# Two operations a tile for the heads of layers 1 and 2, score columns in ScalarE's copy, and new orders of work

## The reference

```
h = jnp.maximum(_layernorm(x), 0.0)
x = x + _L1_gnn_ref(h, adj, W, a)
#   h = (x @ W).reshape(.., 4, 64); e = leaky_relu(s_src[:, :, None] + s_dst[:, None])
#   att = softmax(where(adj > 0, e, MASK)); h_prime = einsum('bijh,bjhd->bihd', att, h)
```

## Time and profile before

| | |
|---|---|
| time, median of 3 runs | 4377.15 us (4377.02 to 4380.96) |
| the profiled execution | 4382.13 us, span 4380.3 us |
| PE busy | 4104.0 us, 94% |
| DVE busy | 3246.0 us, 74% |
| ACT busy | 2163.2 us, 49% |
| POOL busy | 417.4 us, 10% |
| mean granted TensorE clock | 0.969 |

### The profile page before, as it was taken

One profiled execution on the slowest core, in us unless ns is written; L12 is line 12 of the kernel. 1 busy time (PEld: TensorE's weight loads), 2 busy tenths in 40 slices (PEclk: granted clock), 3 DMA queues, 4 the chain that ended last, 5 costly groups with the idle time before them and its releaser, 6 DMA issues.

```text
span 4380.3 us, 59537 instructions
## 1 busy us (share of the span) xinstructions
PE 4104.0 (94%) x22884; PEld 1923.7 (44%) x22884; DVE 3246.0 (74%) x6985; ACT 2163.2 (49%) x3361; POOL 417.4 (10%) x469
## 2 busy tenths in 40 slices
PE   5799999999999999999999999999999999999987
PEld 2344444344444444444444444444444444444443
DVE  5577777877777877777877777877777877777854
ACT  3344455544455544455544455544455544555532
POOL 0001010101110100110100110100110100110100
PEclk9899999999999999999999999999999999999998
DMA  3111211111111111101111111112101121101000
GB/s 101 29 35 54 54 40 34 48 40 54 54 33 41 35 54 54 54 30 44 35 54 54 54 30 44 34 54 54 54 29 45 35 54 54 53 26 39 25 30 29
DMA packets 212314, 193.92 MB, mean 44 GB/s; under 512 B 144448, under 2 KB 179008, under 8 KB 203584
## 3 DMA queue, kind: packets, MB, share of 16 engines
q1 hardware_dynamic: 212032, 190.12, 15.3%
HBM read 138.95 MB, written 17.56 MB: 36 GB/s over the span
## 4 chain that ended last, share of the span: by engine, by line
PE 57%; DVE 30%; ACT 5%; SPq 3%; DMA 2%; issue 2%; POOL 1%; DVEq 0%; ACTq 0%; POOLq 0%
PE M L422 10%; PE M L435 9%; DVE PG L1017 6%; DVE PP L903 6%; PE M L488 5%; PE M L446 4%; DVE x L934 4%; PE O L474 4%; PE S L355 4%; PE O L537 4%; DVE Q L913 4%; DVE PP L1046 3%; PE M L579 3%; PE O L368 2%; SPq L1181 2%
## 5 line engine op out<-in xcount | busy, mean ns | idle before, releaser
L1017 DVE SCALAR_TENSOR_TENSOR PG<-g,tcg,mT 128x512 f32<-128x512 f32 x1024 | 694.3, 743 | 36.0 <-PE O L478 17.0
L622 ACT ACTIVATE PP<-S,reach 128x1024 f32<-128x1024 f32 x512 | 542.4, 1110 | 238.6 <-PE S L355 189.2
L903 DVE TENSOR_TENSOR PP<-PP,mT 128x1024 f32<-128x1024 f32 x512 | 597.7, 1214 | 32.0 <-ACT PP L622 32.0
L474 PE MATMUL O<-PG,V 128*32 128x512 f32 x4096 | 536.5, 643 | 10.7 <-DVE PG L1017 9.3
L647 ACT ACTIVATE z<-x,nb,rs 128x256 f32<-128x256 f32 x384 | 209.2, 597 | 540.1 <-DVE nb L893 540.1
L422 PE MATMUL M<-hT,W 128*128 128x512 f32 x1024 | 456.0, 598 | 5.1 <-ACT hT L657 2.0
L435 PE MATMUL M<-W,H 128*128 128x256 f32 x2048 | 459.7, 378 | 0.0
L1128 POOL TENSOR_SCALAR ve<-mv 128x4 f32<-128x4 f32 x192 | 111.3, 580 | 3409.3 <-DVE mv L861 3409.3
L979 DVE TENSOR_TENSOR x<-x,M 128x256 f32<-128x256 f32 x128 | 52.6, 411 | 490.5 <-PE M L435 490.4
L435 PEld LDWEIGHTS M<-W,H 128*128 128x128 f32 x2048 | 377.3, 189 | 71.6 <-issue 10.6
L355 PE MATMUL S<-hT 32*128 32x512 f32 x2048 | 325.6, 707 | 56.3 <-ACT PP L622 28.4
(11 more groups left out here) (136 smaller groups left out, 5511.2 us busy)
## 6 DMA issues: line engine op xcount, KB each, us to landing
g<-t_rows SPq DMA_DIRECT2D x64, 1024.0 KB, 5.1
adj<-adj_in SPq DMA_DIRECT2D x32, 1024.0 KB, 5.4
x<-x_in SPq DMA_DIRECT2D x32, 512.0 KB, 4.3
z<-t_rows SPq DMA_DIRECT2D x64, 256.0 KB, 4.0
out<-x SPq DMA_DIRECT2D x32, 512.0 KB, 2.9
W<-w_in SPq DMA_DIRECT2D x1, 3072.0 KB, 16.5
mT<-z SPq DMA_TRANSPOSE x128, 3.7
m<-V SPq DMA_TRANSPOSE x128, 2.5
```

The source lines that it names most:

```text
L474: e.matmul(k.O[0][r:r + 32, :], s.V[:, jt, 64 * hh + 32 * v:64 * hh + 32 * v + 32], p[:, u, :], start=(jt == 0), stop=(jt == NT - 1))
L622: e.activation(p[:, 2 * pair:2 * pair + 2, :], k.S[:, 2 * pair:2 * pair + 2, :], ACT.Exp, bias=k.reach[:, 7:8], scale=SC0).then_inc(k.e0.s ...
L903: e.tensor_tensor(p[:, 2 * pair:2 * pair + 2, :], p[:, 2 * pair:2 * pair + 2, :], s.mT[:, jt:jt + 1, :].to_broadcast([128, 2, N]), ALU.mul ...
L1017: e.scalar_tensor_tensor(out=p[:, u, :], in0=s.T[hh], scalar=s.tcg[:, 1, hh, jt:jt + 1], in1=s.mT[:, jt, :], op0=ALU.max, op1=ALU.mult).th ...
```

## The change

The scaled heads of layers 1 and 2 go into V in one instruction a tile, and fin adds V to x in another. V gets 264 columns a row, the last 8 are stt, and ACT's copy of a projected tile takes all 264; DVE's copy is gone. Waits of DVE on itself (diag, zb) use its own chain counter in place of signals. The landings of layers 1 and 2 share a semaphore. The five orders are rewritten: b0 now stands for what was b1, and so on.

```diff
-            s.V = sb(f"V{k}", [128, NT, D])
+            vs = sb(f"V{k}", [128, NT, D + 8])
+            s.V, s.stt = vs[:, :, 0:D], vs[:, :, D:D + 8]
+            s.vs = vs[:, :, :]
-            s.mk = s.V[:, :, :].rearrange("p t d -> p (t d)").bitcast(BF16).rearrange("p (t n) -> p t n", t=NT)
+            s.mk = vs[:, :, :].bitcast(BF16)[:, :, 0:N]
...
+    def nth(self, b, i):
+        return self.sems[b % self.n], 16 * (self.per * (b // self.n) + i + 1)
...
@@ class Pe, b2r
-        self.take(f"M{t % 2}", k.add[L].at(b, t) if L else k.nrm.at(b, t))
+        self.take(f"M{t % 2}", k.nrm[L].at(b, t))
@@ class Pe, pj
-        self.take(f"M{t % 2}", k.pjs[L].at(b, t))
+        self.take(f"M{t % 2}", k.pjc[L].at(b, t))
@@ class Act, pj
-        e.copy(s.V[:, t, :], k.M[t % 2][:, 0:256]).then_inc(k.pjc[L].sem, 1)
+        e.copy(s.vs[:, t, :], k.M[t % 2][:, 0:264]).then_inc(k.pjc[L].sem, 1)
@@ class Dve, b2r
-        if L:
-            for h in range(4):
-                x = s.x[:, t, 64 * h:64 * h + 64]
-                r = e.scalar_tensor_tensor(out=x, in0=M[:, 64 * h:64 * h + 64], scalar=s.ri[:, t, h:h + 1], in1=x,
-                                           op0=ALU.mult, op1=ALU.add)
-            r.then_inc(k.add[L].sem, 1)
-        else:
-            e.tensor_tensor(s.V[:, t, :].rearrange("p (h d) -> p h d", d=32), ...
+        n = 4 if L else 8
+        e.tensor_tensor(s.V[:, t, :].rearrange("p (h d) -> p h d", h=n), M[:, 0:256].rearrange("p (h d) -> p h d", h=n),
+                        s.ri[:, t, 0:n, None].to_broadcast([128, n, D // n]), ALU.mult).then_inc(k.nrm[L].sem, 1)
@@ class Dve, fin
+        self.wait_ge(*k.nrm[L].at(b, t))
+        dst = s.x if L else s.z
+        e.tensor_tensor(dst[:, t, :], dst[:, t, :], s.V[:, t, :], ALU.add).then_inc(k.add[L].sem, 1)
@@ class Dve, pj
-        e.tensor_copy(s.stt[:, t, :], k.M[t % 2][:, 256:264]).then_inc(k.pjs[L].sem, 1)
```

More of the change, by code:

```diff
@@ L1304, in tensor_program @@
+    for it in range(0, NB + 3):
+        b0, b1, b2, b3 = it, it - 1, it - 2, it - 3
+        do.sc0(b1, 3)
+        do.dn0(b1, 0)
+        do.pv0(b1, 2)
         do.qk(b3, 0)
+        do.sc0(b1, 4)
         do.qk(b3, 1)
[L1306 to L1307 removed]
+        do.dn0(b1, 1)
         do.pv0(b1, 3)
[L1309 to L1317 removed]
@@ new lines, in scalar_program @@
+        do.pj(b1, 1, 1)
+        do.pj(b1, 1, 2)
+        do.pj(b1, 1, 3)
+        do.gprep(b1, 1)
+        do.ln1(b0, 0)
+        do.grow(b1, 1)
+        do.gout(b2, 2, 1)
+        do.ln1(b0, 1)
+        do.ln1(b0, 2)
+        do.ln1(b0, 3)
+        do.qt(b0, 0)
+        do.sc0(b0, 0)
+        do.gout(b1, 1, 0)
+        do.qt(b0, 1)
+        do.sc0(b0, 1)
+        do.lnz(b2, 3, 0)
+        do.lnz(b2, 3, 1)
+        do.lnz(b2, 3, 2)
+        do.lnz(b2, 3, 3)
+        do.gout(b1, 1, 1)
+        do.tt(b2, 3, 0)
@@ L1530, in vector_program @@
+        do.tt(b2, 3, 1)
+        do.sc0(b0, 2)
+        do.sc0(b0, 3)
+        do.qk(b2, 0)
+        do.sc0(b0, 4)
+        do.qk(b2, 1)
+        do.out0(b0, 0)
+        do.sc0(b0, 5)
+def vector_program(do):
+    for it in range(0, NB + 3):
+        b0, b1, b2, b3 = it, it - 1, it - 2, it - 3
         do.bst(b2, 4, 2)
+        do.bag(b2, 4, 0)
         do.bst(b2, 4, 3)
-        do.bag(b2, 4, 0)
-        do.bst(b0, 0, 0)
-        do.sc0(b1, 3)
-        do.pa0(b1, 1)
-        do.zb(b1)
-        do.bst(b0, 0, 1)
@@ new lines, in vector_program @@
+        do.bag(b1, 3, 2)
+        do.bag(b0, 1, 2)
+        do.bag(b0, 1, 3)
+        do.bag(b1, 3, 3)
+        do.gw(b2, 2, 1)
+        do.nb(b1, 3)
+        do.gw(b2, 2, 2)
+        do.gw(b2, 2, 3)
+        do.nb(b0, 1)
+        do.gmax(b1, 1)
+        do.rb3(b3)
+        do.gprep(b1, 1)
+        do.gvals(b1, 1)
+        do.zb(b0)
+        do.wo(b3, 0)
+        do.wo(b3, 1)
+        do.rc(b2, 2, 0)
+        do.b2r(b2, 2, 0)
+        do.rc(b2, 2, 1)
+        do.fin(b2, 2, 0)
+        do.b2r(b2, 2, 1)
@@ new lines, in vector_program @@
+        do.rc(b2, 2, 2)
+        do.fin(b2, 2, 1)
+        do.b2r(b2, 2, 2)
+        do.bst(b2, 5, 0)
+        do.rc(b2, 2, 3)
+        do.bag(b2, 5, 0)
+        do.b2r(b2, 2, 3)
+        do.fin(b2, 2, 2)
+        do.gw(b1, 1, 0)
+        do.bst(b2, 5, 1)
+        do.bag(b2, 5, 1)
+        do.gw(b1, 1, 1)
+        do.bst(b2, 5, 2)
+        do.fin(b2, 2, 3)
+        do.bst(b2, 5, 3)
+        do.bag(b2, 5, 2)
+        do.gw(b1, 1, 2)
+        do.bag(b2, 5, 3)
+        do.gw(b1, 1, 3)
+        do.nb(b2, 5)
@@ L1564, in gpsimd_program @@
+        do.sc0(b0, 0)
+        do.sc0(b0, 1)
+        do.pa0(b0, 0)
+        do.rc(b1, 1, 0)
+        do.b2r(b1, 1, 0)
+        do.rc(b1, 1, 1)
+        do.b2r(b1, 1, 1)
+        do.sc0(b0, 2)
+        do.rc(b1, 1, 2)
+        do.b2r(b1, 1, 2)
+        do.rc(b1, 1, 3)
+        do.fin(b1, 1, 0)
+        do.b2r(b1, 1, 3)
+        do.sc0(b0, 3)
+        do.pa0(b0, 1)
+        do.fin(b1, 1, 1)
+        do.bst(b1, 4, 0)
+        do.bst(b1, 4, 1)
+        do.fin(b1, 1, 2)
+        do.fin(b1, 1, 3)
 def gpsimd_program(do):
```

576 lines of the change are left out of this document (237 added, 339 removed).

## The result

The changed kernel takes 4274.32 us (median of 4 runs, 4272.96 to 4274.97) against 4377.34 for the kernel before, measured beside it (4377.02 to 4380.96): a ratio of 0.9762, 95% interval 0.9745 to 0.9779. That is 103 us less; 4293 (84 less) was forecast, in a range of 4240 to 4370.

What follows compares the result with a forecast made beforehand. PE was taken to bound the kernel, through a pass counted about 31 times, with DVE the second bound. The terms summed to -2.7 us a pass, -84 us in all: 4293 us against the median, range 4240 to 4370.

Steps and rivals of the forecast that it cites:

- (a): b2r of layers 1 and 2, scale plus add replacing four DVE instructions a tile: 0.8 us saved a pass, 0 to 1.2.
- (b): Projection columns: DVE loses eight copies, ACT copies 264 columns for 256; 0.2 us of PE a pass, bounds 0 and 0.6.
- (c): Signals turned into marks and shared landing semaphores: same instructions and same waits, so 0.
- (d): End of the pass in new orders, from wo to the scores: 1.6 us less a pass, bounds 0 and -2.3.
- (e): PE's clock dip after layer 2's b2r, gone in most passes: -2.9 us a pass, bounds 0 and -3.4.
- (g): DVE's lead through layer 0 is too small, so PE gives time back: +1.3 us a pass, bounds 0 and 3.
- (f): New waits from moved steps, such as layer 3's tt and layer 0's b2r: +0.9 us a pass, bounds 0.2 and 3.
- Fill and drain: Start and end of the span, outside the equal passes: -10 to +15 us, taken as 0.
- the first: The clock dip after layer 2's b2r stays: -1.1 us a pass, 4343 us; chance 0.22.
- Rival 4: Nothing gained: DVE's and ACT's chain through layer 0 takes all, 4377 us; chance 0.07.
- Rival 3: Slower: gw and nb(5) late on DVE, gpv and layer 3's tt wait; +1.9 us a pass, 4436 us; chance 0.09.

## Why the prediction was right, and where it was not

The direction, the size within a quarter and the shape were right: passes shorter by 3.3 us (2.7 predicted), transposes closer together, scores at full clock in most passes, DVE as what is late next. The mechanism behind the largest term was wrong, and the sum came out close by luck: two errors of opposite sign met. One premise was too strong as well, that DVE waits for PE only in the MLP. In the trace of before it also waits 2.4 us a pass for wo's product and 0.5 ahead of gw.

- **(a), its own size right, its effect too small.** The step summed instruction times, 0.8 us a tile going to 0.67 to 0.82, and took 0.8 a pass for eight tiles (its upper bound of 1.2 does not follow from these, 8 x 0.13 = 1.0 does). Inside the new orders DVE's time in these steps fell by just that, 7.8 to 7.0 us a pass. But the two operations bring DVE's last sum forward by 52.1 - 50.6 = 1.5 us, and are worth 43 us in the old orders and 52 to 60 in the new ones (1.4 to 1.9 a pass; 1.4 with the clock at 1.00 in both). In the new orders the other part is DVE's wait of 0.79 us in layer 0, which went with them. In the old ones DVE's time in these steps fell from 7.2 to 6.4 and its wait for PE ahead of gw from 0.5 to 0.1; the rest was not found. (a) had no term for a wait of DVE.
- **(b), too small for the new orders.** 0.2 predicted with 0.6 as its upper bound; 0.9 measured, with the copies at the place that the run gave them. The bound priced M's release by the copy's length, 0.16 us. The cost was the queue ahead of the copy, a pair of masks and an nb that waits: 1.15 us. In the old orders even 0.2 would have been too much. The stride of V cost nothing, as taken.
- **(c)**, taken as 0, had no run of its own. Its waits are in every kernel with the new orders; the chain counter is also in the kernel with the two operations alone.
- **(d), about right.** Wo's wait is 0.43 to 0.44 as worked out, but the row it was compared with (0.87) was not typical: over all passes before, that wait was 17.3 us in 30 times, 0.58. From wo's start to the scores: 8.9 predicted, 8.71 without a dip and 9.05 with one. zb was late as predicted, and did not cost its 0.45, as the run with zb early shows.
- **(e), the step that failed.** The dip was priced at the 2.9 us that it costs PE. It was worth 0.5 a pass in the kernel before (0.8 at most), 0.35 with four operations in the new orders, and nothing in the kernel after. And it is not gone "in most passes" by much: 11 of 29 still have it, at no cost. (g) was meant to correct this, giving 1.3 back to DVE's lead; (e) and (g) together said -1.6 a pass, and the runs say -0.5 (-0.8 at most). The lead was counted at layer 0's end only, and it is used up at once: gw follows directly behind b2r on DVE, and the first value matmuls after the scores already wait for it (2.03 us for 1.92 with the clock at 1.00).
- **(f), within its bounds, in other places.** 1.36 instead of 0.9: 0.45 and 0.63 at layer 1's third b2r and the fourth scores (0.3 predicted for both), 0.28 in w1, against 0.38 that went at the eighth scores; none visible at layer 3's tt and none at layer 0's first b2r (0.3 each predicted).
- **(g), right as a mechanism.** Extra DVE work between wo and layer 0's end costs 80% of its length, the same kind of work in the MLP nothing.
- **Fill and drain:** 14 us less, 0 predicted with -10 as the bound, so outside it. The fill is unchanged. The drain, from the last batch's first scores on, is 289.1 us before, 280.6 with the new orders alone, 283.9 with the two operations alone and 275.1 after: both shorten it. What does so inside it was not looked at.

Of the rivals, the first (the dip stays, 4343) had a premise that was nearer to what the runs show, that the dip hardly counts for the kernel's time. Its number missed because it took (a) and (b) as they stood. Rival 4, a chain through layer 0 that takes all, named the right chain but had the change leave it as long as it was. Rival 3, a slow gw, appears as 0.3 and 0.5 us at the first two value blocks, not as 3 a pass.

## What to carry to other kernels

Before pricing lost clock or idle time of the busiest engine, look at what the engine behind it does in the same stretch: if that has no gap, the time is hidden, and dummy work in the idle places measures it in one run. Price an instruction by where it stands in its queue and by the buffer that it holds, not only by its own length. When a run puts a part back, its place in the order is part of what is measured: the copies were free at one place and cost 28 us at another.
